# Local attention layers: the token shift behind each output projection made by two SBUF-to-SBUF transfers

## What is computed

```python
def shift_tokens(t):
    a, s = jnp.split(t, 2, -1)
    s = jnp.pad(s, ((0, 0), (1, 0), (0, 0)))[:, :-1]
    return jnp.concatenate([a, s], -1)
...
for i in range(DEPTH):          # DEPTH = 6
    x = attn_layer(shift_tokens(x), Wqkv[i], q_scale[i], k_scale[i], Wo[i]) + x
    x = ffn_layer(shift_tokens(x), ln_g[i], ln_b[i], W1[i], b1[i], W2[i], b2[i]) + x
```

## Time and profile before

| what | value |
|---|---|
| median of 3 runs | 4612.93 us (4612.48 to 4614.09) |
| profiled execution, span from first to last instruction | 4612.9 us |
| busy: PE, DVE, ACT, POOL | 92%, 81%, 76%, 69% of the span |
| mean granted TensorE clock | 0.959 |
| shift matmul, its copy on ACT, the low-half copy on POOL | 192 of each (32 sequences, 6 layers) |

### The profile page before, as it was taken

The page is one execution under the profiler, slowest core; times in us unless marked ns, Lnnn a source line. Parts: engine busy times, 40 slices in busy tenths (PEclk is TensorE's granted clock), DMA queues, the critical chain, the costliest instruction groups (busy, mean ns, idle before and its releaser), DMA issues. The chain is left out here.

```text
span 4612.9 us, 154012 instructions
## 1 busy us (share of the span) xinstructions
PE 4249.6 (92%) x51351; PEld 2797.3 (61%) x51353; DVE 3755.0 (81%) x9044; ACT 3499.8 (76%) x12855; POOL 3200.2 (69%) x4297
## 2 busy tenths in 40 slices
PE   6949999999999999999999999999999999777885
PEld 3426656665666656666566665666656666455543
DVE  4779899994999849997599966999669995688497
ACT  6948788883888838898488875888658886588434
POOL 2522299993999839997499975999659995344162
PEclk8969999999999999999999999999999999788986
DMA  2000000000000000000000000000000000000000
GB/s 62 0 21 1 6 2 0 0 1 25 2 0 0 1 25 2 0 0 19 7 2 0 0 20 6 2 0 0 20 7 1 0 0 20 1 0 0 28 0 19
DMA packets 36135, 34.48 MB, mean 7 GB/s; under 512 B 11302, under 2 KB 31012, under 8 KB 34852
## 3 DMA queue, kind: packets, MB, share of 16 engines
q1 hardware_dynamic: 35876, 31.13, 2.2%
HBM read 29.03 MB, written 2.10 MB: 7 GB/s over the span
## 5 line engine op out<-in xcount | busy, mean ns | idle before, releaser
L2238 ACT ACTIVATE local_prob<-ps,local_shift_by 128x128 f32<-128x128 f32 x3072 | 1078.5, 377 | 3.3 <-DVE local_shift_by L2330 3.2
L2166 POOL TENSOR_TENSOR local_qk<-local_qk,local_rsin 128x512 f32<-128x512 f32 x768 | 968.0, 1271 | 43.4 <-DVE local_rsin L2355 43.4
L2173 POOL TENSOR_TENSOR local_qk<-local_qk,local_inv 128x512 f32<-128x512 f32 x768 | 792.3, 1043 | 131.2 <-ACT local_inv L2257 130.5
L2497 PE MATMUL ps<-local_wqkv,local_xsT 128*128 128x512 f32 x1536 | 798.4, 604 | 10.6 <-DVE local_rsin L2355 5.2
L2180 POOL TENSOR_TENSOR local_prob<-local_prob,local_rs 128x512 f32<-128x512 f32 x768 | 789.9, 1040 | 12.2 <-DVE local_rs L2337 12.2
L2238 ACT ACTIVATION_READ_ACCUMULATOR local_prob<-ps,local_shift_by 128x1 f32 x3072 | 671.9, 219 | 0.0
L2330 DVE TENSOR_REDUCE local_shift_by<-ps 128x4 f32<-128x512 f32 x768 | 524.8, 683 | 81.3 <-PE ps L2575 80.8
L2355 DVE TENSOR_TENSOR local_rsin<-ps,local_sin_t 128x256 f32<-128x256 f32 x1536 | 572.0, 414 | 0.0
L2344 DVE TENSOR_TENSOR local_qk<-ps,local_cos_t 128x512 f32<-128x512 f32 x768 | 525.2, 684 | 35.8 <-ACT local_sq L2246 34.4
L2246 ACT ACTIVATE local_sq<-ps 128x512 f32<-128x512 f32 x768 | 466.7, 608 | 76.7 <-PE ps L2497 38.9
L2362 DVE TENSOR_REDUCE local_ss<-local_sq 128x8 f32<-128x512 f32 x768 | 513.3, 670 | 4.0 <-ACT local_sq L2246 4.0
(11 more groups left out here) (338 smaller groups left out, 8768.6 us busy)
## 6 DMA issues: line engine op xcount, KB each, us to landing
local_wqkv<-L_ffn_Wqkv SPq DMA_DIRECT2D x7, 1536.0 KB, 6.2
local_wo<-L_ffn_Wo SPq DMA_DIRECT2D x7, 512.0 KB, 7.0
out<-quantised_res SPq DMA_DIRECT2D x8, 256.0 KB, 2.3
local_w<-L_ffn_W SPq DMA_DIRECT2D x6, 341.0 KB
early_L_decay<-c_decay SPq DMA_DIRECT2D x1, 1024.0 KB, 10.7
local_w<-L_ffn_W SPq DMA_DIRECT2D x12, 64.0 KB
load_raw<-L_ffn_w SPq DMA_DIRECT2D x8, 64.0 KB, 2.0
local_b<-L_ffn_b SPq DMA_DIRECT2D x24, 0.5 KB
```

Of the source, the lines that this page charges most:

```text
L2166: nc.gpsimd.tensor_tensor(qk[w][:, j, :, :], qk[w][:, j, :, :], rsin[j % 2][:, :, :], ALU.add).then_inc(rot_ready, 1)
L2173: nc.gpsimd.tensor_tensor(qk[w][:, j, :, :], qk[w][:, j, :, :], bcast(inv[:, w, 8 * j:8 * j + 8].unsqueeze(2), [P, 8, LH]), ALU.mult).then ...
L2238: last = nc.scalar.activation(prob[w][:, g, j, :], ps[:, 4 + g % 2, j * P:(j + 1) * P], ACT.Exp, bias=shift_by[:, w, h:h + 1], accum_out=s ...
L2497: nc.tensor.matmul(proj_bank(j), xsT[w][:, :], wqkv[:, 512 * j:512 * j + 512], start=True, stop=True).then_inc(proj_ready, 1)
```

## The change

The shift matmul on PE, the copy `high_half` on ACT and the copy `low_half` on POOL go. SP issues two transfers for each sequence instead: features 64 to 127 of tokens 0 to 126 of `xnew` to tokens 1 to 127 of `xs` (127 rows of 256 bytes), and features 0 to 63 of all 128 tokens (128 rows of 256 bytes). It issues them when `residual` of b and `norm` of b - 2 are done. One semaphore for each of the two buffers counts both transfers; `statistics` waits for it, and `residual` waits for that of two sequences earlier. Row 0 of the shifted half is zeroed once per layer on DVE.

```diff
-    half_ready = sem("half_ready")
-    shift_turned = sem("shift_turned")
-    shift_ready = sem("shift_ready")
+    shifted = [sem(f"shifted{u}") for u in range(2)]
...
             load_ffn_weights(sp, env, a, layer)
 
+            def shift_tokens(b, w, live):
+                if live(b):
+                    waits_alone(sp, env, (xnew_ready, b + 1), (xn_ready, b - 1))
+                    sp.dma_start(xs[1:P, w, LH:P], xnew[0:P - 1, w, LH:P]).then_inc(shifted[w], 16)
+                    sp.dma_start(xs[:, w, 0:LH], xnew[:, w, 0:LH]).then_inc(shifted[w], 16)
+
+            def step(n, u, live):
+                shift_tokens(n, u, live)
+            sequence_loop(sp, NB, 0, 0, step)
...
-            def low_half(b, w, live):
-                if live(b):
-                    wait_alone(pool, env, xnew_ready, b + 1)
-                    wait_alone(pool, env, xn_ready, b - 1)
-                    nc.gpsimd.tensor_copy(xs[:, w, 0:LH], xnew[:, w, 0:LH]).then_inc(half_ready, 1)
...
-            def high_half(b, w, live):
-                if live(b):
-                    act.wait_ge(shift_turned, b + 1)
-                    wait(act, xn_ready, b - 1)
-                    nc.scalar.activation(xs[:, w, LH:P], OUT[:, 2 * P:2 * P + LH], ACT.Copy).then_inc(shift_ready, 1)
...
             nc.vector.memset(ss[:, :, :, 1:2], 1e-24)
+            nc.vector.memset(xs[0:1, :, LH:P], 0.0)
...
                     dve.wait_ge(out_ready, b + 1)
                     wait(dve, x_ready, b - 1)
-                    wait(dve, half_ready, b - 1)
-                    wait(dve, shift_turned, b - 1)
+                    wait(dve, shifted[w], 16 * (b - w))
                     nc.vector.tensor_tensor(xnew[:, w, :], X[:, bass.ds(b * P, P)], OUT[:, 0:P], ALU.add).then_inc(xnew_ready, 1)
...
-                    wait_alone(dve, env, half_ready, b + 1)
-                    wait_alone(dve, env, shift_ready, b + 1)
+                    wait_alone(dve, env, shifted[w], 16 * (b - w) + 32)
                     nc.vector.bn_stats(stats[:, w, :], xs[:, w, :]).then_inc(stats_ready, 1)
...
-            def shift(b, w, live):
-                if live(b):
-                    pe.wait_ge(xnew_ready, b + 1)
-                    wait(pe, xsT_ready, upto(b + 6, NB))
-                    if isinstance(b, int):
-                        wait(pe, xnew_ready, b + 1)
-                        wait(pe, shift_ready, b)
-                    nc.tensor.matmul(OUT[:, 2 * P:2 * P + LH], env["shift"][:, :], xnew[:, w, LH:P],
-                                     start=True, stop=True).then_inc(shift_turned, 1)
...
                 project(n, u, 0, live)
-                shift(n - 5, v, live)
                 project(n, u, 1, live)
```

More of the change, by code:

```diff
@@ L2192, in step @@
                 normalise(n - 4, u, 1, live)
-                low_half(n - 6, u, live)
                 rotate(n - 2, u, 3, live)
@@ L2291, in step @@
                 log_norms(n + 4, u, live)
-                high_half(n, u, live)
                 over_norms(n + 4, u, live)
@@ L2463, in turn_x @@
                     if isinstance(b, int):
-                        wait(pe, shift_ready, b - 5)
                         wait(pe, xsT_ready, b)
```

## The result

| | before | after |
|---|---|---|
| median | 4612.93 us (4612.48 to 4614.09) | 4645.49 us (4636.62 to 4650.86) |
| ratio to before | | 1.0068 [1.0056, 1.0081] |
| the profiled execution: its span | 4612.9 us | 4640.4 us |

The change costs 0.68% by the ratio of the runs and 32.6 us by the medians, where 22 us had been forecast; the range held the time. The runs of the changed kernel lie 14 us apart, those of the kernel before 1.6.

What follows compares the result with a forecast made beforehand. PE was taken to bound steady attention steps, and a latency chain of PE, DVE and ACT the block ends. 4612.9 - 24.3 (PE) + 39.4 (block ends) + 7.2 (clock) = 4635 us; range 4597 to 4662.

Steps and rivals of the forecast that it cites:

- PE's saving: Steady attention steps: removing the shift matmul saves PE about 0.15 us a step over 162 steps, 24.3 us.
- 0.05 us of the 0.16 come back as a new wait: Steady step, `project(2)`: PE arrives earlier but waits for DVE's second `sines`, with 0.11 us of room; 0.05 us lost.
- The shorter wait of `turn_x`: First step of each turn: `residual` starts sooner, so `turn_x` waits 0.07 us less, 0.035 us a step.
- L: Time from `residual`'s start until DVE can start `statistics`: 5.0 us, hidden in steady steps under 9.26 us of room.
- The end of a block: Sequences 29 to 31: L lies open, delays 1.02, 1.85 and 3.70 us add up, 39.4 us for six layers.
- the slacks of 0.66 us: Block end, behind the first two of the last three residuals: DVE idles 0.66 us before `evacuate_heads`, so `statistics` has that slack.
- The clock: Start of feed-forward blocks: PE's longer pause brings the clock to 0.50, 1.2 us each, 7.2 us for six.
- The first: Rival: the 127 rows spread over all engines, L = 2.9, 4598 us if the clock holds; chance 0.20.
- The second: Rival: L near 4.1 and the clock holds, block ends cost 23.2 against 24.3 us saved, 4612 us; chance 0.13.
- The third: Rival: DVE or POOL holds the steady step by another chain, nothing is saved, 4659 us; chance 0.09.
- the wait at `residual`: Argument against the third rival: DVE waits for PE at `residual` in both steps of a turn.
- The fourth: Rival: a row costs over 52 ns on one engine, L passes its room, steady steps stall, 4913 us; chance 0.03.

Runs made afterwards that it cites:

- half evacuation: Changed kernel with DVE copying only 256 of 512 columns of its half of the value projection; 4626.68 us in a single run.
- dummy matmul: Changed kernel with a 128x64 matmul, result unread, at the shift's old place on PE; 4635.46 us in a single run.
- the reordered kernels: Values moved ahead of keys in PE, DVE and ACT lists: with transfers up to sequence 28, copies for the last three, 4650.67 us; in the kernel before, 4654.13 us.
- the fillers: Changed kernel with 26 filler matmuls in place of 8 at the end of each attention block; 4630.81 us, 1.0039 of the kernel before.
- the run with 128 rows: Changed kernel with its 127-row transfer made 128 rows, without the shift by a token; 4621.18 us, 1.0015 of the kernel before.
- transfers in steady steps: Changed kernel with sequences 29 to 31 back on shift matmul and two copies, all others by transfer; 4608.27 us, 0.9988 of the kernel before.

## Why the prediction was right in sign and range, and where it was not

**PE's saving: the step that failed.** Predicted 0.16 - 0.05 + 0.035, about 0.15 us a step and 24.3 us; measured 0.073 and 11.8 (162 steps), of which 9.9 show in the table, whose 27 steps a layer include the first ones. The failed step is "0.05 us of the 0.16 come back as a new wait". I looked for the next wait that the trace of before shows, the one of `project(2)`, and found its room about right (0.11, by the half evacuation 0.09). But `project(1)` needs a bank that DVE is still emptying, and the shift had covered that exactly: 834.93 to 835.62 before, with the next load at 835.70. 0.136 us of 0.167 turn into this wait, 0.03 stay, and `project(2)` is reached too little earlier to wait longer. Half evacuation and dummy matmul agree; the reordered kernels lost the wait and still got slower, at another place, and do not test it. The saving would have been larger by 0.08 us with the evacuation out of the way, not by 0.13, since `project(2)` then takes its share.

**The shorter wait of `turn_x`.** Predicted 0.035 us a step. The first step of a turn went from 0.936 + 0.233 us (`project(3)`, `turn_x`) to 0.861 + 0.204, 0.10 less, 0.05 a step: right, and a bit small. It is the larger part of what PE gained.

**L.** Predicted 5.0 us, measured 4.2: start right (0.63 us for 0.6), one engine for 127 rows right, but 14 ns a row where I took 20 between 13 and 26. That is 0.76 us and all of the difference. The last packet of the pair comes 3.2 us behind the issue of the 127 rows, where a landing near 4 us had been named. L was hidden in steady steps, as forecast.

**The end of a block.** By the prediction's own formula with L = 4.2: 0.22 + 1.05 + 2.90 = 4.17 us a layer, 25.0 in all; measured 6.9 from output 27 to 31, and 17.2 behind output 31 (2.87 a layer, at the full clock), 24.1 in all. So the slacks of 0.66 us and the sum of delays were right; the 39.4 us were too much only through L.

**The clock.** Predicted 7.2 us at the start of feed-forward blocks; measured 7.5 for five, as forecast from the earlier trace rows (behind the sixth come other stages, which are in the table's 7.7), and the fillers show it alone. Two more costs were not in the sum: 6.0 us at the last output projection (1.5 in four layers), and about 2.5 at the starts of attention blocks. The pauses for a transfer lie ahead of the last output projection too, and I had priced only the seam. That the spread of the runs comes from how often the clock falls is likely: one layer shows these falls and another doesn't, and the five runs stand in the order of their mean granted clock (0.959 at 4636.62 us, 0.958, 0.956, 0.955, 0.954 at 4650.86). Only one of them has a trace, so where the others fall is not shown.

**The sum.** -11.8 + 24.1 + 7.5 + 8.5 is 28.3 us over the kernel before. The stretches that the change touches are 30.4 us longer by the spans; the 1.9 us between 11.8 and 9.9 are most of the rest. That the sum comes near the 27.5 of the whole spans is luck, since 2.9 us of those are gained in stages without the change. The saving was 12.5 us too high, the end of blocks 15 too high, the clock 9 too low. The forecast of 4635 is near because its errors partly cancel, which is luck too.

**The rivals.** The first is excluded by L, and the run with 128 rows shows that its time would not have come with its L either. The second had L nearly right (4.1) and failed on the clock and on the saving of 24.3. The third named the right mechanism, another chain of DVE, which takes half of the saving and not all of it; I argued it away with the wait at `residual`, which says nothing of `project(1)`. The fourth is excluded, 14 ns a row.

## What to carry to other kernels

When an operation leaves a busy engine, list every buffer that the operation behind it writes, and when each comes free: a wait that is hidden under the removed operation shows as no idle time in the trace before. Latency that steady steps hide is paid at every end of a pipeline, so a mixed form is worth a try: the slow path in the steady part, the short one for the last few. Here that was 0.12% faster than the kernel before. A pause of PE cost more than its length here: behind 4.29 us of idle each feed-forward block took 1.45 us more at the lower clock.

## What the runs showed of the hardware

- A transfer from SBUF to SBUF of 127 rows of 256 bytes trickles at 18 GB/s, 14 ns a row; one of 128 rows is over in two slices, 0.35 us. L falls from 4.2 to 3.05 us with the one row more. The trace has one packet of 4 bytes for the first and 16 for the second.
- From its issue a transfer of 32 KB within SBUF over many engines lands in 1.8 us (median of both in the run with 128 rows), as long as the load of `ident` from HBM (64 KB).
- The issue on SP takes longer than I had worked out from loads (0.45 us each): 0.62 us for 127 rows and 0.87 for the 128 behind them; 0.53 for 112 rows, 0.82 for the 15 behind them, and 0.55 for the 128 behind those. Two of 128 rows took 0.47 and 0.60. The second transfer is dearer than the first each time, by how much depends on the pair; why was not found.
- DVE's `norm` (128x128 float32, all in SBUF) showed 0.31 to 1.05 us. Where one of GpSimd's 128x512 operations within SBUF ran at its start and went on for over 0.3 us, `norm` ended 0.08 to 0.09 us behind it, in all places of five traces (before, changed, transfers in steady steps, both reordered). The mechanism was not tested.
